# Loads of the experts' rows issued from ScalarE's queue instead of the sync engine's

## The reference, cut to what matters

```python
x = x + attention(layernorm(x), ctx)              # 16384 tokens, 256 channels
y = layernorm(x)
shared = (silu(y @ sfc1.T) * (y @ sfc2.T)) @ sfc3.T
top_w, top_idx = top_k(y @ gate_w.T, 2)           # of 16 experts
wk = softmax(top_w)
moe = sum over the two experts e of  wk[e] * (silu(y @ w1[e].T) @ w2[e].T)
out = x + shared + moe
```

## Time and profile before

| | |
|---|---|
| median of 3 runs | 1809.21 us (1805.57 to 1814.83) |
| the profiled execution, its own time | 1798.85 us |
| its span, first to last instruction | 1797.0 us |
| mean granted TensorE clock | 0.943 |
| TensorE matmul, weight load | 83%, 73% of the span busy |
| GpSimd, VectorE, ScalarE | 75%, 74%, 40% |

### The profile page before, as it was taken

How to read it: one execution, slowest core, us unless ns; L and a number is a source line. 1 busy time by engine, 2 the same in 40 slices (tenths; PEclk the granted TensorE clock), 3 DMA queues, 4 the chain that set the end, 5 groups by cost and what they waited for, 6 DMA issues and landing times.

```text
span 1797.0 us, 50631 instructions
## 1 busy us (share of the span) xinstructions
PE 1490.8 (83%) x17109; PEld 1307.6 (73%) x17110; DVE 1325.6 (74%) x3306; ACT 725.3 (40%) x1346; POOL 1345.8 (75%) x1253
## 2 busy tenths in 40 slices
PE   5499999999999999999999999987576676676774
PEld 4488888778887788777887787866566676566764
DVE  6587888888888888888888888886355555455553
ACT  3244454444544445444544444433133333233331
POOL 4277777787877777777787877776678888788786
PEclk9699999999999999999999999998699989898886
DMA  8788888888888888889888888774777777677673
GB/s 203 135 210 177 178 172 196 204 174 178 164 208 194 175 174 185 209 177 175 173 196 202 172 181 172 180 166 188 238 226 226 234 224 233 178 230 225 213 227 103
DMA packets 945834, 344.75 MB, mean 192 GB/s; under 512 B 824088, under 2 KB 898730, under 8 KB 940288
## 3 DMA queue, kind: packets, MB, share of 16 engines
q1 hardware_dynamic: 901680, 216.53, 58.6%
q0 software_dynamic: 33600, 92.91, 14.6%
q10 hardware_dynamic: 10512, 34.79, 6.1%
HBM read 200.37 MB, written 148.15 MB: 194 GB/s over the span
## 4 chain that ended last, share of the span: by engine, by line
PE 38%; DVE 17%; issue 16%; SPq 12%; POOL 6%; DMA 6%; ACT 4%; DVEq 0%; POOLq 0%; ACTq 0%
SPq L337 3%; PE bank_a L1171 3%; ACT xn L631 3%; DVE w_sb L786 3%; SPq L331 3%; PE bank_y L1158 3%; PE bank_y L1156 3%; PE bank_y L1157 3%; PE bank_a L1310 3%; PE bank_a L1156 3%; PE bank_z L1156 2%; DVE ln_stats L915 2%; PE bank_a L1158 2%; PE bank_a L1157 2%; PE bank_u L1156 2%
## 5 line engine op out<-in xcount | busy, mean ns | idle before, releaser
L400 POOL DMA_INDIRECT slots<-xn,slot_i x256 | 280.9, 1097 | 96.8 <-issue 54.9
L1111 DVE SCALAR_TENSOR_TENSOR v_area<-bank_y,tail,v_area 128x256 f32<-128x256 f32 x288 | 124.0, 479 | 211.6 <-PE bank_y L1158 95.6
L1399 PE MATMUL bank_a<-ident,k_area 128*128 128x128 f32 x576 | 91.1, 309 | 122.1 <-DMA k_area<-slots 121.1
L521 POOL DMA_INDIRECT sums<-v_area,tail x144 | 144.9, 1006 | 52.2 <-issue 33.3
L521 POOL DMA_INDIRECT out<-v_area,tail x144 | 144.5, 1004 | 50.8 <-issue 33.6
L1399 PEld LDWEIGHTS bank_a<-ident,k_area 128*128 128x128 f32 x576 | 72.6, 158 | 133.6 <-DMA k_area<-slots 132.9
L409 POOL DMA_INDIRECT sums<-v_area,slot_i x128 | 128.0, 1000 | 33.2 <-issue 29.9
L1156 PE MATMUL bank_y<-wsh_out_hi,hid_hi 128*128 128x256 f32 x512 | 143.2, 280 | 1.3 <-POOL hid_lo L431 1.3
L1157 PE MATMUL bank_y<-wsh_out_lo,hid_hi 128*128 128x256 f32 x512 | 143.0, 279 | 0.0
L1158 PE MATMUL bank_y<-wsh_out_hi,hid_lo 128*128 128x256 f32 x512 | 142.8, 279 | 0.0
L701 ACT ACTIVATE k_area<-bank_a 128x512 f32<-128x512 f32 x144 | 80.5, 596 | 143.7 <-PE bank_a L1399 84.5
(11 more groups left out here) (222 smaller groups left out, 5266.7 us busy)
## 6 DMA issues: line engine op xcount, KB each, us to landing
k_area<-slots SPq DMA_DIRECT2D x288, 129.0 KB
v_area<-sums SPq DMA_DIRECT2D x288, 128.0 KB
kv_dram<-w_sb SPq DMA_DIRECT2D x32, 1024.0 KB
x_sb<-in_x_in SPq DMA_DIRECT2D x32, 512.0 KB
ctx_sb<-in_ctx_t SPq DMA_DIRECT2D x32, 512.0 KB
q_dram<-q_sb SPq DMA_DIRECT2D x32, 512.0 KB
k_area<-kv_dram SPq DMA_DIRECT2D x256, 64.0 KB
w_sb<-q_dram SPq DMA_DIRECT2D x256, 64.0 KB
```

The source lines that it names most:

```text
L400: pool.indirect_dma_start(slots[j], bass.IndirectOffsetOnAxis(ap=slot_i[:, par, j, i:i + 1], axis=0), row_of[j][:, i, :], None).then_inc(S ...
L521: pool.indirect_dma_start(target, bass.IndirectOffsetOnAxis(ap=tail[:, r, t, 1 - j:2 - j].bitcast(u32), axis=0), y_ring[:, r, t, :], None, ...
L1111: st = nc.vector.scalar_tensor_tensor(out=y_ring[:, r, t, :], in0=Y[t // 2][:, t % 2 * C:(t % 2 + 1) * C], scalar=tail[:, r, t, j:j + 1], ...
L1399: last = nc.tensor.transpose(A[t // 2][:, t % 2 * C + k * P:t % 2 * C + (k + 1) * P], x_ring[:, r, t, CHANNEL[j] + k * P:CHANNEL[j] + (k + ...
```

## The change

SP no longer loads rows; it loads sums alone, with its own reading of the rows' places. ScalarE issues the loads of rows on its own queue. It issues the first four groups ahead of its first `tiles_out`, and in each group n, behind the rounding of n, the four loads of group n + 4; the wait for `tail_ready` goes with them. ScalarE's loop is cut in two, since the loads of groups 36 on read the other slots. The waits ahead of the first loads (plan ready, padding and scatters landed) move with them.

```diff
@@ sync
-            def load_x(j, n, r, at_rows, first):
-                if not first:
-                    sp.wait_ge(S["tail_ready"], at(1, n - 4, 1))
-                    sp.sem_inc(S["slot_free"], 1)
-                for t in range(4):
-                    sp.dma_start(x_ring[:, r, t, :], slots[j][bass.ds(at_rows[t], P), :]).then_inc(S[f"loaded{r}"], 16)
-            def load_sums(j, n, r, at_rows, first):
+            def load_sums(j, n, r, first):
+                at_rows = tile_rows(n, r)
...
             with sp.Fori(4, QUADS - 3, 4) as q:
                 for r in range(4):
-                    at_rows = tile_rows(q + r, r)
-                    load_x(FIRST, q + r, r, at_rows, False)
-                    load_sums(FIRST, q + r, r, at_rows, False)
-            sp.wait_ge(S["scattered0"], 16 * BPC * CHUNKS)
-            second_rows = [tile_rows(QUADS + r, r) for r in range(4)]
-            for r in range(4):
-                load_x(SECOND, QUADS + r, r, second_rows[r], False)
+                    load_sums(FIRST, q + r, r, False)
             for r in range(4):
                 sp.wait_ge(S[f"added{r}"], 16 * QUADS)
...
@@ scalar
+            def load_x(j, n, r, first):
+                act.reg_load(x_regs[r], slot_row[0:1, bass.ds(n * 4, 4)])
+                if not first:
+                    act.wait_ge(S["tail_ready"], at(1, n - 4, 1))
+                    act.sem_inc(S["slot_free"], 1)
+                for t in range(4):
+                    row = act.snap(x_regs[r][t], min_val=0, max_val=NO_TILE)
+                    act.dma_start(x_ring[:, r, t, :], slots[j][bass.ds(row, P), :]).then_inc(S[f"loaded{r}"], 16)
+
-            def quad(n, r, before_this, last):
+            def quad(n, r, j, before_this, last):
                 expert_tanh(n, r % 2, before_this < 2)
                 if not last:
                     tiles_out(n + 1)
                 e_round(n, r % 2, before_this < 2)
+                if j is not None:
+                    load_x(j, n + 4, r, False)
 
             act.wait_ge(S["o_full"], 2 * CHUNKS)
             act.wait_ge(S["hid_split"], SB * CHUNKS)
+            act.wait_ge(S["rows_ready"], 1)
+            act.wait_ge(S["no_tile_stored"], 2 * 16 * TOP)
+            act.wait_ge(S["padded1"], 2 * 16 * 3)
+            act.wait_ge(S["scattered1"], 16 * BPC * CHUNKS)
+            for q in range(4):
+                load_x(FIRST, q, q, True)
             tiles_out(0)
             for q in range(4):
-                quad(q, q, q, False)
-            with act.Fori(4, TOP * QUADS - 7, 4) as q:
+                quad(q, q, FIRST, q, False)
+            with act.Fori(4, QUADS - 7, 4) as q:
                 for r in range(4):
-                    quad(q + r, r, 4, False)
+                    quad(q + r, r, FIRST, 4, False)
+            act.wait_ge(S["scattered0"], 16 * BPC * CHUNKS)
+            act.wait_ge(S["padded0"], 2 * 16 * 3)
+            with act.Fori(QUADS - 4, TOP * QUADS - 7, 4) as q:
+                for r in range(4):
+                    quad(q + r, r, SECOND, QUADS, False)
             for q in range(TOP * QUADS - 4, TOP * QUADS):
-                quad(q, q % 4, q, q == TOP * QUADS - 1)
+                quad(q, q % 4, None, q, q == TOP * QUADS - 1)
```

More of the change, by code:

```diff
@@ L341, in _ @@
             sp.wait_ge(S["padded1"], 2 * 16 * 3)
[L342 to L345, removed]
             sp.wait_ge(S["based"], 16 * BPC * CHUNKS)
@@ L348, in _ @@
             for q in range(4):
-                load_sums(FIRST, q, q, first_rows[q], True)
+                load_sums(FIRST, q, q, True)
             with sp.Fori(4, QUADS - 3, 4) as q:
                 for r in range(4):
-                    at_rows = tile_rows(q + r, r)
-                    load_x(FIRST, q + r, r, at_rows, False)
-                    load_sums(FIRST, q + r, r, at_rows, False)
-            sp.wait_ge(S["scattered0"], 16 * BPC * CHUNKS)
-            second_rows = [tile_rows(QUADS + r, r) for r in range(4)]
-            for r in range(4):
-                load_x(SECOND, QUADS + r, r, second_rows[r], False)
+                    load_sums(FIRST, q + r, r, False)
             for r in range(4):
@@ L361, in _ @@
             for r in range(4):
-                load_sums(SECOND, QUADS + r, r, second_rows[r], True)
+                load_sums(SECOND, QUADS + r, r, True)
             with sp.Fori(QUADS + 4, TOP * QUADS - 3, 4) as q:
                 for r in range(4):
-                    at_rows = tile_rows(q + r, r)
-                    load_x(SECOND, q + r, r, at_rows, False)
-                    load_sums(SECOND, q + r, r, at_rows, False)
+                    load_sums(SECOND, q + r, r, False)
         @block.gpsimd
@@ L715, in e_round @@
                 nc.scalar.activation(e_hi[:, par, :], e_hid[:, par, :], ACT.Copy).then_inc(S["e_hi_ready"], 1)
-            def quad(n, r, before_this, last):
+            x_regs = [[act.alloc_register(f"x_row{r}_{t}") for t in range(4)] for r in range(4)]
+            def load_x(j, n, r, first):
[7 more added lines that the diff above has]
+            def quad(n, r, j, before_this, last):
                 expert_tanh(n, r % 2, before_this < 2)
```

## The result

The changed kernel takes **1793.05 us** (median of 7 runs, 1792.0 to 1797.12), the kernel before 1809.21 us (1805.57 to 1815.1 in its 7 runs beside it): a ratio of 0.9911, 95% interval 0.9895 to 0.9927. Its profiled execution took 1792.32 us, with a span of 1790.5, against 1798.85 and 1797.0. The spans differ by 6.5 us where the medians differ by 16.2, so the profiles have to be split into their parts.

What follows compares the result with a forecast made beforehand. GpSimd was taken as the floor, 6.52 us per group, with waits for late rows above it. Terms -17.3 + 2 + 1.3 = -14 us gave 1809.2 - 14 = 1795 us; forecast's range 1789 to 1800, whole range 1786 to 1814.

Steps and rivals of the forecast that it cites:

- the 2 us kept for late tanhs: Second phase, steady part: 2 us allowed for groups where ScalarE's tanh comes late because of its added issuing.
- the start: Start of the second phase: early rows of groups 4 and 5 beside the padding writes cost 1.3 us, bounds 0 and 2.6.
- the change of halves: Between the second phase's halves: the 6.28 us wait, ruled by writes and sums, stays; worth 0.
- The excess over GpSimd's floor: Steady part of the second phase: 6.87 us per group against a floor of 6.52; 17.3 us can be won.
- strong end: The forecast's best case: -20 us, with up to 3 us of GpSimd's other delays won too; 1789 us.
- SP and the transfers: Second phase: SP's four fewer issues per group are worth nothing by themselves; bytes stay the same and the DMA engines have room.
- Rival (b): Second phase: transfers are the bound, 6.95 us per group at 227 GB/s, so the time stays at 1809; chance 0.09.
- ScalarE's issues: Each group: ScalarE's batch of four loads takes 1.8 to 2.4 us, its cycle 4.2 to 6.75; free under 6.52.
- Rival (c): Between rounding and next tanh: ScalarE held at its four loads; +28 us, 1837, deciding from 3.5 us per batch; chance 0.13.
- the rival's lower values: ScalarE's cycle under (c): 1.45 from tanh to rounding plus 0.95 to the first load, with a 3.9 us batch 6.3.
- Rival (a): Second phase: something else is late next, TensorE or ScalarE's tanh; gain 0 to 8 us, 1801 to 1809; chance 0.22.
- Phase one: Before the first padding write: a time changed by more than 1 us would be against the whole forecast and its rivals.

## Why the prediction was right, and where its terms were off

The forecast was 1795 us, a gain of 14; the median is 1793.05, a gain of 16.2 (20.8 on the other chip), and 17.0 in the second phase of the profiles. The mechanism came as forecast; part of the closeness is luck, since terms were off against each other: the halves won 3.4 us more and the 2 us kept for late tanhs weren't needed, while the start cost 1.9 us more and the change of halves 0.4.

- *The excess over GpSimd's floor.* Right, and the floor of 6.52 us too: the groups went to 6.51 and 6.54, and the added instruction shows that nothing else bounds the changed kernel. The term was 17.3 us and measured 20.7 (20.4 between the two profiles shown first). The trace of the kernel before accounts for it. Of the 22.7 us of extra waits there about 1.6 lie ahead of the stretch that was read: the third group took 8.06 us and takes 6.56 now. In the stretch they are some 21, since the term took the waits with a named releaser alone and left out nearly 4 us that the view marks "issue", most of it 2.7 us in three gaps between two writes; the prediction had kept up to 3 us of such delays for its strong end. All of the 22.7 are gone, and GpSimd's instructions take 2.7 us more in sum (the remainder 783 ns against 771), which leaves 20.0. GpSimd's waits for VectorE, 24.7 us, were to fall to 8 to 10 and are 7.1; TensorE's for rows were to fall under 10 and are 0.
- *The 2 us kept for late tanhs.* This term was wrong by all of it. With the rows issued 15.3 us early no rounding is waited for (2.1 us before) and no tanh comes too late.
- *The start.* The mechanism was right, the size too small: +1.3 was taken with 2.6 as the bound; it measured 3.2 on the mean, 1.5 to 4.7 between pairs of profiles. The first sums were forecast at 1288.4 to 1291; less the 9.1 us of phase one they stand at 1292.8. Keeping the early rows clear of the padding gave 2.4 us back between two profiles of one chip, so the collision is the main part. The bound priced two batches by their own bytes at 404 GB/s; why they hold the padding up for longer than that was not followed.
- *SP and the transfers.* Worth nothing, as said. Rival (b) fell: 238 GB/s at a DMA share of 0.76 where it was 227 at 0.75, with the pace at the floor. The Trainium skill (DMA: Bandwidth & Descriptors, "Issuing engines are not separate DMA queues") holds here in one half: SP alone in the other order came to 0.9921, ScalarE's queue without the early order to 0.9995, so a second queue as such brought nothing at this pace. The other half, that only the starting engine's time is saved, leaves out what this change is worth: a queue's loads stand behind each other's waits.
- *ScalarE's issues.* The batches took 1.92 us, inside the 1.8 to 2.4; the cycle came to some 4.1 us, just under the 4.2 to 6.75 and far from the middle of 5.4. Rival (c) didn't show: both queues issue four loads per group, and neither was held up near the 3.5 us from which it decides. From group 6 on the 48 batches that run beside one of SP's for 0.8 us or more took 1.93 us on the mean, the six beside none 1.88. Where a batch did reach 5.09 us, the price was there: the rival's lower values, 1.45 + 0.95 + 5.09, give 7.49 us per group, and 7.49 and 7.31 were measured; that this is so close is luck, the parts being others (7.30 in the timeline). With the 2.2 us that ScalarE really needs beside its issues (1.45 + 0.66 + 0.11) the rival would decide from a batch of 6.87 - 2.2 = 4.7 us only. The lock of the Trainium skill (Perfetto Trace Analysis, "DMA Instruction — HWDGE (DVE, Sync)") is thus not seen on ScalarE at this density, nor at the doubled one, where the higher price is the halves' own. On SP's side a small one isn't excluded: in the kernel with doubled issues its batches of sums took 2.25 us beside ScalarE's and 1.94 in the four beside none.
- *Rival (a)* fell: TensorE without waits for rows and GpSimd without waits for VectorE came together.
- *The change of halves* was put at 0 and measured +0.4 us. *Phase one* was to stay within 1 us, or be against all of it. It differed by 9.1 us, and this criterion was wrong: it took one execution's phase one as fixed, where the same kernel shows 1244.1 and 1251.3. The forecast carried the 10.4 us between the profiled execution and the median over unexplained; phases one with and without dips differ by about as much.

## What to carry to other kernels

A load that waits in a queue also waits for whatever its neighbours wait for: compare the time at which its buffer came free with the time at which it was issued, and if there is a gap, change the order of issue first. A second queue helped here for the same reason only: nothing beyond another order at 6.5 us per group, 9.8 us where the one queue no longer kept the rows early. The room for it is the slack of the engine that issues, here some 0.5 us per load of 128 rows and 0.65 per load of 64. Loads that can now go early should be followed to the first place where the DMA engines are full.

## What the runs showed of the hardware that was not expected

- In some executions, of either kernel, TensorE's granted clock falls to half for 3.4 us at a time, again and again in phase one. Eight to twelve such dips between 160 and 1200 us go with a phase one of 1251 to 1260 us, none with 1240 to 1246; all but one of the profiles with them are of one chip, and that one's isn't known. Two profiles can therefore differ by 10 us where the change has no part, and medians or the changed phase alone have to be compared.
- A load of 64 rows cost ScalarE 0.64 us to issue, one of 128 rows 0.48, with SP issuing beside it or not.
- Taking 0.95 us per group off the busiest engine made the kernel slower, with the granted clock at 0.83 instead of 0.94 in the same stretch and starts that no record explains.
